# Twelve layer norms regrouped over four engines and fused with six projections, and the 16-head attention exponentials kept in PSUM

## What is computed

```python
def _layernorm(x, axis=-1, eps=1e-05):
    m = jnp.mean(x, axis=axis, keepdims=True)
    v = jnp.var(x, axis=axis, keepdims=True)
    return (x - m) / jnp.sqrt(v + eps)
...
x = x + _L0_xattn_ref(_layernorm(x), ctx_1024, ctx_1024, ...)   # 16 heads of depth 8, causal
x = x + _L0_attn_ref(_layernorm(x), ...)                        # a decaying scan, two projections
x = x + _L0_ffn_ref(_layernorm(x), ...)                         # sparse experts
...
x = x + _L2_attn_ref(_layernorm(x), ...)                        # gated scan, two projections
...
x = x + _L3_attn_ref(_layernorm(x), ...)                        # 16 heads of depth 8
x = x + _L3_ffn_ref(_layernorm(x), ...)                         # sparse experts
```

## Time and profile before

| | |
|---|---|
| median of 3 runs | 3825.92 us (3824.61 to 3829.24) |
| the profiled execution | 3828.19 us |
| its span | 3825.7 us, 102951 instructions |
| mean granted TensorE clock | 0.857 |
| PE busy | 2837.8 us (74%) |
| DVE busy | 2580.4 us (67%) |
| ACT busy | 1654.5 us (43%) |
| POOL busy | 1453.3 us (38%) |
| DMA | 226.54 MB, mean 59 GB/s |

### The profile page before, as it was taken

One profiled execution on the slowest core, in us unless ns is written; L12 is line 12 of the kernel. 1 busy time (PEld: TensorE's weight loads), 2 busy tenths in 40 slices (PEclk: granted clock), 3 DMA queues, 4 the chain that ended last, 5 costly groups with the idle time before them and its releaser, 6 DMA issues. The chain is left out here.

```text
span 3825.7 us, 102951 instructions
## 1 busy us (share of the span) xinstructions
PE 2837.8 (74%) x27568; PEld 2246.5 (59%) x27569; DVE 2580.4 (67%) x9045; ACT 1654.5 (43%) x5099; POOL 1453.3 (38%) x1363
## 2 busy tenths in 40 slices
PE   5872378659999788657999972248839999967662
PEld 3651377537777677534777751247727777746562
DVE  5977521268888845556888885662158888869635
ACT  1112034337777622224777765204317777711111
POOL 1520057525655400002555540007615555525252
PEclk9985589879999989878999995559969999979765
DMA  2000244511111000201232310204524444300122
GB/s 80 0 0 14 91 119 141 138 37 36 35 36 35 24 1 0 94 12 43 70 70 69 70 39 0 53 18 144 132 77 107 104 103 103 89 1 0 33 78 73
DMA packets 213222, 226.54 MB, mean 59 GB/s; under 512 B 31235, under 2 KB 180739, under 8 KB 212452
## 3 DMA queue, kind: packets, MB, share of 16 engines
q1 hardware_dynamic: 200452, 199.44, 19.6%
q0 software_dynamic: 12672, 25.98, 2.6%
HBM read 202.77 MB, written 22.55 MB: 59 GB/s over the span
## 5 line engine op out<-in xcount | busy, mean ns | idle before, releaser
L1656 POOL TENSOR_TENSOR sx<-sx,rs 128x1028 f32<-128x1028 f32 x384 | 732.1, 1906 | 589.8 <-DVE rs L1787 589.8
L1735 ACT ACTIVATE sx<-sx,nm 128x257 f32<-128x257 f32 x1536 | 770.7, 505 | 349.1 <-DVE nm L1781 349.1
L1781 DVE CUSTOM_DVE_ANT_0 sx<-bank,rows 128x257 f32<-128x257 f32 x1024 | 394.0, 422 | 78.7 <-PE bank L1725 73.7
L1408 ACT ACTIVATE hT<-bank,B 128x128 f32<-128x128 f32 x714 | 206.1, 368 | 324.6 <-PE bank L1376 322.8
L1735 ACT ACTIVATION_READ_ACCUMULATOR sx<-sx,nm 128x1 f32 x1536 | 290.5, 189 | 0.0
L1725 PE MATMUL bank<-kT,qb 32*128 32x257 f32 x3072 | 276.0, 428 | 3.6 <-DVE nm L1781 3.6
L1797 DVE COPY pt<-bank 128x512 f32<-128x512 f32 x384 | 263.3, 686 | 4.6 <-PE bank L1676 4.6
L1676 PE MATMUL bank<-C,sx 128*128 128x128 f32 x1536 | 251.9, 286 | 3.4 <-DVE a L1830 3.4
L1434 DVE TENSOR_TENSOR yb<-bank,b2s 128x128 f32<-128x128 f32 x159 | 46.3, 291 | 302.1 <-PE bank L1389 298.2
L1714 PE MATMUL bank<-pt,vs 128*32 128x128 f32 x6144 | 247.4, 279 | 0.0
L1688 PE MATMUL bank<-ct,W 128*128 128x257 f32 x768 | 234.8, 388 | 17.0 <-DVEq L1768 15.5
(11 more groups left out here) (385 smaller groups left out, 6337.0 us busy)
## 6 DMA issues: line engine op xcount, KB each, us to landing
ct<-in_ctxT SPq DMA_DIRECT2D x384, 128.5 KB
W<-in_L_w SPq DMA_DIRECT2D x159, 256.0 KB
rows<-rows_x SPq DMA_DIRECT2D x256, 128.5 KB
keep<-rows_keep SPq DMA_DIRECT2D x128, 128.5 KB
yg<-copy_outs SPq DMA_DIRECT2D x40, 256.0 KB
token_rows<-XN SPq DMA_DIRECT2D x24, 256.0 KB, 2.3
vl<-last_v SPq DMA_DIRECT2D x384, 2.0 KB
W<-in_L_w SPq DMA_DIRECT2D x39, 128.0 KB
```

The lines of the kernel that those rows point to most:

```text
L1656: pool.tensor_tensor(sx[:, j, :, 0:KEYS], sx[:, j, :, 0:KEYS], rs[:, j, :].unsqueeze(2).to_broadcast([P, 4, KEYS]), ALU.mult).then_inc(p_r ...
L1735: ins = act.activation(sx[:, j, h, 0:KEYS], sx[:, j, h, 0:KEYS], ACT.Exp, bias=nm[:, j, h:h + 1], scale=-1.0, accum_out=sm[:, j, h:h + 1])
L1781: dve.tensor_tensor_reduce(sx[:, j, h, 0:KEYS], B[h][:, 0:KEYS], add, -1.0, 3.0e38, ALU.add, ALU.min, nm[:, j, h:h + 1]).then_inc(s_summed ...
```

## The change

1. The norm makes its statistics in two halves of 16 tiles. After each half POOL computes var to the power of -0.5 (a tensor_tensor with `ALU.pow` on 128x16), and DVE makes -mean*rstd (`nmr`). ACT no longer computes the root.
2. Normalising is split: ACT does groups 0 to NA-1 as `Identity(rstd * x + nmr)`, with NA = 5 or 6, DVE the remaining ones. All normalised tiles have a place of their own. PE and ACT turn and copy as before; everything is written out, without loops.
3. Where the projection's input is `XNT` (six of the seven projections), it moves into the norm's block: PE multiplies group g right after turning group g+1, into banks 2 to 7; ACT evacuates job 1 two groups later, DVE jobs 0 and 2.
4. With `add_back`, DVE adds after its own groups.
5. In `attn16` scores have four banks; maximum, subtraction and exponential are done in the bank, and the normalised probabilities go to `e` in SBUF. The head selection moves from DVE to ACT as four 128x128 operations with bias and scale from SBUF. The values are transposed straight from `VT`, one tile ahead, and the addition to `X` is for tile t-3 and stands between the subtraction and the row sum. All stages are written out.

```diff
-        def norm(add_back=False, XN=None, fetch=None):
+        def norm(add_back=False, XN=None, fetch=None, jobs=()):
+                HT = TILES // 2
+                NA = (5, 6, 5, 6)[len(jobs)]
...
-                xn = hold(c2, "xn", [P, 2, GT, P]) if XN is None else XN[:].rearrange("p (g j) d -> p g j d", j=GT)
+                xn = hold(c2, "xn", [P, TILES, P]) if XN is None else XN
...
+                @block.gpsimd
+                def _(pool):
+                    for h in range(2):
+                        hs = slice(h * HT, (h + 1) * HT)
+                        pool.wait_ge(*var_ready(h + 1))
+                        pool.tensor_tensor(rstd[:, hs], var[:, hs], nhalf[:], ALU.pow).then_inc(rstd_ready.sem, 1)
...
+                    for h in range(2):
+                        hs = slice(h * HT, (h + 1) * HT)
+                        dve.wait_ge(*rstd_ready(h + 1))
+                        ins = dve.scalar_tensor_tensor(out=nmr[:, hs], in0=mean[:, hs], scalar=-1.0, in1=rstd[:, hs],
+                                                       op0=ALU.mult, op1=ALU.mult)
+                        ins.then_inc(stat_ready.sem, 1)
+                    for k in range(GROUPS):
+                        if NA + k < GROUPS:
...
+                        for j in (0, 2):
+                            if j < len(jobs):
+                                to, wt, frm, bias, scale = jobs[j]
+                                dve.wait_ge(*psum[j](k + 1))
+                                dve.tensor_scalar(to[:, k * GW:(k + 1) * GW], B[2 + 2 * j + k % 2][:], bias, scale,
+                                                  ALU.add, ALU.mult).then_inc(done[j].sem, 1)
...
                 def _(act):
-                    act.wait_ge(*var_ready(1))
-                    st_.link(act.activation(var[:], var[:], ACT.Ln))
-                    act.activation(rstd[:], var[:], ACT.Exp, scale=-0.5).then_inc(rstd_ready.sem, 1)
...
+                    for k in range(GROUPS + 3):
+                        if k < NA:
+                            act.wait_ge(*stat_ready(1 if k < GROUPS // 2 else 2))
+                            for t in range(k * GT, (k + 1) * GT):
+                                ins = act.activation(xn[:, t, :], X[:, t, :], ACT.Identity, bias=nmr[:, t:t + 1], scale=rstd[:, t:t + 1])
+                            ins.then_inc(xa_ready.sem, 1)
+                        g = k - 1
+                        if 0 <= g < GROUPS:
+                            act.wait_ge(*xnT_psum(g + 1))
+                            act.copy(XNT[:, g * GW:(g + 1) * GW], B[g % 2][:]).then_inc(xnT_ready.sem, 1)
...
                 def _(pe):
+                    for k in range(GROUPS + 1):
+                        if k < GROUPS:
+                            wait_normed(pe, k)
+                            pe.wait_ge(*xnT_ready(k - 1))
+                            for j in range(GT):
+                                ins = pe.transpose(B[k % 2][:, j * P:(j + 1) * P], xn[:, k * GT + j, :], ident)
+                            ins.then_inc(xnT_psum.sem, 1)
+                        g = k - 1
+                        if g >= 0 and jobs:
+                            pe.wait_ge(*xnT_ready(g + 1))
+                            for j, (to, wt, frm, bias, scale) in enumerate(jobs):
+                                pe.wait_ge(*done[j](g - 1))
+                                pe.matmul(B[2 + 2 * j + g % 2][:], wt, frm[:, g * GW:(g + 1) * GW],
+                                          start=True, stop=True).then_inc(psum[j].sem, 1)
...
         def attn16(name, src, bv, bo, causal):
...
-                            pe.wait_ge(*centred(t - 1))
+                            pe.wait_ge(*e_normed(t - 3))
...
                 def _(act):
-                        act.wait_ge(*centred(t + 1))
-                        act.activation(e[:, q, :], e[:, q, :], ACT.Exp).then_inc(exp_ready.sem, 1)
+                        if ok(t):
+                            act.wait_ge(*centred(t + 1))
+                            act.activation(SB[t % 4][:], SB[t % 4][:], ACT.Exp).then_inc(exp_ready.sem, 1)
+                        u, z = t - 1, 1 - q
+                        if ok(u):
...
+                            act.wait_ge(*av_psum(u + 1))
+                            act.wait_ge(*y_psum(u - 1))
+                            for j in range(4):
+                                ins = act.activation(m[:, z, j, :], B[2 + z][:, j * P:(j + 1) * P], ACT.Identity,
+                                                     bias=bvh[:, j:j + 1], scale=const("head")[:, j:j + 1])
+                            ins.then_inc(heads_ready.sem, 1)
...
                 def _(dve):
...
-                            st_.link(dve.tensor_copy(vt[:, q, :], VT[:, tok]))
-                            dve.transpose(vt[:, q, :], vt[:, q, :]).then_inc(v_turned.sem, 1)
+                            if t == 0:
+                                turn(t, q)
                             dve.wait_ge(*scores(t + 1))
...
-                            dve.wait_ge(*av_psum(u + 1))
-                            dve.wait_ge(*y_psum(u - 1))
-                            dve.scalar_tensor_tensor(out=m[:, z].rearrange("p j t -> p (j t)"), in0=B[2 + z][:],
-                                                     scalar=v(bv), in1=const("diag512"), op0=ALU.add,
-                                                     op1=ALU.mult).then_inc(heads_ready.sem, 1)
...
+                        u, z = t - 3, 1 - q
                         if ok(u):
                             dve.wait_ge(*y_psum(u + 1))
                             xt_ = X[:, bass.ds(u, 1), :]
                             dve.tensor_tensor(xt_, xt_, B[4 + z][:, 0:P].unsqueeze(1), ALU.add).then_inc(x_added.sem, 1)
-                    run(dve, stages, 2, st_, 10)
+                        if ok(t + 1):
+                            turn(t + 1, 1 - q)
+                        if ok(t):
+                            dve.wait_ge(*exp_ready(t + 1))
...
```

More of the change, by code:

```diff
@@ L236, in groups, with wait_normed, _ @@
+                psum = [sig(f"proj_psum{j}", GROUPS) for j in range(len(jobs))]
+                done = [sig(f"proj_done{j}", GROUPS) for j in range(len(jobs))]
+                kept = sig("rows_kept", GROUPS if XN is not None else 0)
+                block = c2.enter_context(nc.Block())
+                def wait_normed(eng, g):
+                    eng.wait_ge(*(xa_ready(g + 1) if g < NA else xd_ready(g - NA + 1)))
+                @block.sync
+                def _(sp):
                     if XN is not None:
+                        rows = T["token_rows"].rearrange("(t p) d -> p t d", p=P)
@@ L237, in groups @@
                         for g in range(GROUPS):
[L238 to L242 removed]
+                            wait_normed(sp, g)
+                            sp.dma_start(rows[:, g * GT:(g + 1) * GT, :], XN[:, g * GT:(g + 1) * GT, :]).then_inc(kept.sem, 16)
@@ L281, in _ @@
+                    if add_back:
+                        for g in range(GROUPS):
+                            wait_normed(dve, g)
+                            xg = X[:, g * GT:(g + 1) * GT, :]
+                            st_.count(dve.tensor_tensor(xg, xg, xn[:, g * GT:(g + 1) * GT, :], ALU.add))
                     st_.close()
@@ L295, in _ @@
-                    groups(act, turned)
+                    for k in range(GROUPS + 3):
[8 more added lines that the diff above has]
+                            act.copy(XNT[:, g * GW:(g + 1) * GW], B[g % 2][:]).then_inc(xnT_ready.sem, 1)
+                        g = k - 3
+                        if len(jobs) > 1 and 0 <= g < GROUPS:
+                            to, wt, frm, bias, scale = jobs[1]
+                            assert scale == 1.0
+                            act.wait_ge(*psum[1](g + 1))
+                            act.activation(to[:, g * GW:(g + 1) * GW], B[4 + g % 2][:], ACT.Identity, bias=bias).then_inc(done[1].sem, 1)
@@ L2015, in program @@
             attn16("x0", ctx0, "x0_bv", "x0_bo", True)
-        norm()
         rwkv()
```

171 lines of the change are left out of this document (66 added, 105 removed).

## The result

The changed kernel took 3703.11 us (median of 4 runs, 3696.64 to 3715.05) against 3827.58 us for the kernel before (4 runs): a ratio of 0.9678, 95% interval 0.9651 to 0.9704. Measured again beside later kernels on another chip the ratio was 0.9686 (0.9669 to 0.9702).

The account below looks back on a forecast made before the run. No engine is full overall; DVE bounds the 16-head attentions, dependency chains the norms. 3828.2 - 40 (attention) - 38 (fused norms) + 5 (other norms) + 1 (tables) = 3756.2 profiled, 3754 median; range 3740 to 3772, with rivals 3728 to 3795.

Parts of the forecast that it names:

- The chain through the exponential: 16-head attentions: DVE's dependent steps from maximum to transposes sum to 4.50 us a tile, period taken as 4.55.
- rival 3: Attention: period does not fall to 4.55 us, through PSUM writes, handing over or PE in step; +14 us, chance 15%.
- Rival 5: Both attentions: straight-line code stalls on fetching by 1 us a tile, eating 64 us; nothing moves beyond noise; chance 4%.
- the split that a rule spoke against: Attention's head selection as four ACT operations: the rule of tiles of 512 or more makes it lose 0.8 us a tile.
- The new activations: ACT's 128-column operations with two operands from SBUF: 0.38 us each in a row, 1.55 for a group of four.
- Rival 2: Norms: POOL's power is slow, costing from 5 us and cancelling the gain at 7.5; ends slower; chance 8%.
- DVE waits on rstd over 1 us: Norms: a sign that would show the prediction wrong, DVE held up by POOL's root for over 1 us.
- 9.9 us after the first statistic instead of 11.1: Norms' start: when ACT begins its first group, given the root made in halves; a gain of 1.2 us.
- PE turns a group in ... 0.66: Fused norms: PE's time to turn one group, 1.09 us at 1.2 GHz and 0.66 at 2.4.
- I let it rise after the second group: Fused norms: PE's clock, dense with work inside the norm, goes up from 1.2 GHz after the second group.
- Rival 1: Fused norms: PE's clock stays at 0.50, one-job norms take 37 us instead of 29.7; +31 us, chance 15%.
- Rival 4: Norms go better than counted, with PE at 2.4 GHz from the start; 3740 us, chance 10%.

Follow-up runs that it names:

- e4: The kernel before with only the loop of the 16-head attention written out; ratio to the kernel before 0.9984, -5 us.
- e11: The changed kernel with the head selection back on DVE as one 512-column operation between subtraction and addition; ratio to the kernel before 0.9726.
- e7: The changed kernel with the root on ACT again, for all 32 tiles after both halves of the statistics; ratio to the kernel before 0.9731.
- e3: The kernel before with the loops of norm and projection written out, nothing else changed; ratio to the kernel before 0.9837, -61 us.
- e6: The changed kernel with every projection in its own written-out block behind its norm; ratio to the kernel before 0.9778.
- e5: The changed kernel with ACT normalising 3 groups instead of 5 without jobs, 4 instead of 6 with one; ratio to the kernel before 0.9639.
- e9: The kernel before, loops kept, with 96 transposes of the identity on PE at the head of each norm; ratio to the kernel before 0.9983.
- e13: The kernel before with norm and projection written out, plus three 384-column DVE memsets as pauses in each norm; ratio to the kernel before 0.9901.

## Why the prediction missed, step by step

**Attention: right in mechanism, 9 us short.** The chain through the exponential is the bound, as argued, and neither POOL nor ACT is. The period was put at 4.55 us and is 4.41 in a3 and 4.51 on average in x0. The exponential in PSUM takes 0.58 us, not 0.63; row sum to transposes 1.74, not 1.79; and I had added 0.05 for a semaphore that costs nothing. In x0, where PE needs 4.41 us a tile by the earlier trace rows, every second maximum waits for PE's scores, hence 4.44 and 4.58 in turn: PE is in step with DVE, rival 3 in a mild form. The 1.5 us for start and end of each block did not show; they are 3 of the 9. Rival 5's stalls did not come either: writing the blocks out made e4 faster. And the split that a rule spoke against gained: ACT's four parts take 1.50 us where DVE's one took 0.74, yet e11 shows 0.34 us a tile for it, as ACT works 2.1 us of 4.41.

**The new activations: right.** 0.38 us each was predicted; four take 1.65 us with the last one's tail, eight 3.19, so 0.39 apart. My 1.55 for a group left part of that tail out.

**The root: right, with a price that was unknown.** 2.9 us against my 1; under the 4.7 from which it would have counted. Rival 2 began at 5 and needed 7.5. My sign "DVE waits on rstd over 1 us" did come, 2.93 us in each norm, and was badly chosen: with a price of 2.9 that wait lies where nothing needs DVE yet, and e7 shows that the root on POOL gains all the same.

**The start: mis-sized by 1.5 us a norm.** ACT starts 8.38 us after the first statistic, not 9.9. I took over the statistics' pace from a loop, where two register operations stand ahead of each: from the first statistic to the small operations it is 7.78 us looped and 6.32 in e3, which only writes the loops out. That is nearly all of the 1.5. Over 12 norms this is some 18 us of the 51. It is the step "9.9 us after the first statistic instead of 11.1".

**Fused norms: -63 where -38 were counted.** One-job stages came out at 25.9 for 29.7, two-job ones at 30.9 and 31.8 for 34.6, a3's at 37.6 for 42.2. The start is 1.5 of each. Two terms make up most of the 1.3 to 3.1 us that are left, both PE's. The first is "PE turns a group in ... 0.66" taken as time on the path: 0.22 of it is the tail, which the projection overlaps. So groups come every 1.30, 2.16 and 3.02 us with one, two and three jobs, where I had 1.52, 2.38 and 3.24; over six groups that is 1.3 us. The second is "I let it rise after the second group", by which I made the first group's projection cold. With two and three jobs the clock rose within it: three projections took 3.12 us in a3's stage where three at 1.2 GHz are 5.2, and two took 2.5 instead of 3.4. In the one-job stages the first projection was cold as counted (1.92 us), and ACT's groups, at 2.01 us for 2.1, give the other half us. Rival 1, the clock staying at 0.50, did not come; e6 shows that it does come without the fusion. Rival 4 had the direction, but gave it 14 us and another reason: PE was not at 2.4 GHz from the start, it turned its first two groups in 1.11 us each.

**Other norms: -10 where +5 was counted.** The start again, 1.5 us each, is 9 of the 15. The rest is for the most part the end: in the norm alone ACT's last group was ready 17.6 us after the first statistic and the last copy done at 21.9, where I had 19.5 and 24.6. The sign of the argument was right for all that: e3 and e5 show that ScalarE's five groups make these norms 2 us longer than VectorE alone would.

**The step that was missing.** The prediction lists "everything is written out, without loops" as part of the change and gives it no price; it appears only as a risk, in rival 5. The trace had the price: pauses of 0.24 us between the halves of the statistics and of 0.45 us before PE's groups, with the granted clock of 0.50 beside them. e3 puts it at 61 us, half of the whole result. These 61 are not a part of the miss of 51 to be added to the terms above: for the fused norms I had counted a risen clock without seeing that the loops were what had kept it down. The miss itself is 9 us in the attention, 25 in the fused norms, 15 in the others and 2 elsewhere.

## What to carry to other kernels

A loop around short operations has a price in two places: the engine that issues them, and TensorE, whose clock may stay at its lower level on account of pauses of 0.4 us; read the granted clock of each stage and ask what keeps it down. When a rewrite changes the structure and also writes out loops, cost the writing out as an edit of its own, and try it alone first: here it was the simplest half of the gain, and in five further places (two scans, the 8-head attention, x0's projection, the last norm) it gave more. Where the issuing engine has no pauses, as in the 16-head attention, it gave 5 us. Moving work to an idle engine may slow the stage if its pace is worse (ScalarE's group of 2.0 us against VectorE's 1.1); it pays where a third engine has other work to put into the pauses.

## What the runs showed of the hardware

- GpSimd's power on 128x16 took 2.90 to 2.93 us in all 24 cases, 0.18 us a column if none of it is fixed (only this width ran); its product of 128x128 took 0.40 in all.
- An exponential of 512 columns in place took 0.58 us in PSUM and 0.63 in SBUF.
- TensorE with its clock at 2.4 GHz, turning groups of 0.65 us with pauses of 0.4 to 1.2 us between them, was back at 1.2 GHz after four groups (e9); with 4.28 us of work in 4.7 us its clock rose (e3), with pauses of 0.4 us between stretches of 2.14 it did not in 10 us (e13).
- Sixteen `bn_stats` on 128 columns: 3.75 us from a loop with register addresses, 3.18 with fixed ones.
- Two matmul operations that follow each other overlap: a group's four transposes show 0.60 us in the row, and the projection behind them starts 0.44 us after their start (the ends of such rows are modelled, the starts are not).
